# Attention: row sums in the maxima's banks, three banks for scores, maxima one at a time and later in a tile

## What is computed

```python
q = rms_norm(x @ w_q.T + b_q, g_q)        # 512 x 32
k, v         # 1344 text rows, masked beyond a length
k_img, v_img # 257 image rows
def attention(q, k, v, mask=None):
    s = einsum('bqhd,bkhd->bhqk', q, k) * SCALE
    p = softmax(where(mask, s, -1e9), axis=-1)
    return einsum('bhqk,bkhd->bqhd', p, v)
out = attention(q, k, v, mask) + attention(q, k_img, v_img)
```

## Time and profile before

| | us |
|---|---|
| median of three runs | 3357.7 |
| profiled execution | 3349.82 |
| its span, first to last instruction | 3347.8 |
| PE busy | 3063.8 |
| DVE busy | 2053.6 |
| ACT busy | 1606.9 |
| POOL busy | 1376.9 |

### The profile page before, as it was taken

The page is one execution under the profiler, slowest core; times in us unless marked ns, Lnnn a source line. Parts: engine busy times, 40 slices in busy tenths (PEclk is TensorE's granted clock), DMA queues, the critical chain, the costliest instruction groups (busy, mean ns, idle before and its releaser), DMA issues. The chain is left out here.

```text
span 3347.8 us, 49752 instructions
## 1 busy us (share of the span) xinstructions
PE 3063.8 (92%) x15756; PEld 1888.5 (56%) x15756; DVE 2053.6 (61%) x3425; ACT 1606.9 (48%) x3005; POOL 1376.9 (41%) x545
## 2 busy tenths in 40 slices
PE   7999999999599999999999999999994488999991
PEld 6777777777344444444444444444441466777771
DVE  5666766666566666766766666667652774443435
ACT  3343433434166666666666666666663653222222
POOL 0000000000087787877877877778775161000000
PEclk9999999999599999999999999999996699999996
DMA  5666667676846466465565564664633361000005
GB/s 170 157 163 166 163 162 169 160 150 159 169 83 132 104 127 126 97 128 124 107 133 106 125 132 99 125 127 100 133 55 108 93 203 44 1 1 0 0 0 201
DMA packets 374881, 385.16 MB, mean 115 GB/s; under 512 B 47792, under 2 KB 297712, under 8 KB 368504
## 3 DMA queue, kind: packets, MB, share of 16 engines
q1 hardware_dynamic: 363272, 323.61, 40.7%
q0 software_dynamic: 7168, 50.34, 8.5%
q10 hardware_dynamic: 4224, 8.39, 0.7%
HBM read 210.77 MB, written 121.15 MB: 99 GB/s over the span
## 5 line engine op out<-in xcount | busy, mean ns | idle before, releaser
L962 ACT ACTIVATE at_probs<-at_st 128x512 f32<-128x512 f32 (+1 forms) x1664 | 914.0, 595 | 614.5 <-PE at_st L812 599.0
L992 DVE TENSOR_REDUCE at_cm<-at_mx 128x2 f32<-128x896 f32 x768 | 813.1, 1087 | 432.1 <-PE at_mx L828 432.1
L772 POOL TENSOR_TENSOR at_added<-at_added,at_probs 128x2048 f32<-128x2048 f32 x192 | 888.6, 4628 | 11.5
L812 PE MATMUL at_st<-at_qst,at_kst 101*128 101x512 f32 (+1 forms) x1664 | 656.0, 456 | 6.2 <-ACT at_probs L962 5.7
L812 PEld LDWEIGHTS at_st<-at_qst,at_kst 101*128 101x128 f32 (+1 forms) x1664 | 265.9, 184 | 597.4 <-ACT at_probs L962 454.1
L828 PE MATMUL at_mx<-at_kst,at_qst 97*128 97x448 f32 (+1 forms) x2048 | 530.1, 362 | 50.1 <-DMA at_kst<-stack_rows 23.2
L850 PE MATMUL at_acc<-at_probs,at_vt 128*32 128x512 f32 (+2 forms) x3584 | 478.3, 608 | 0.7 <-ACT at_probs L962 0.7
L828 PEld LDWEIGHTS at_mx<-at_kst,at_qst 97*128 97x128 f32 x2048 | 371.3, 194 | 158.6 <-DVE at_cm L992 77.4
L740 POOL MEMSET at_ones<- 128x32 f32 x1 | 0.1, 130 | 819.1 <-POOLq L302 819.1
L772 POOL TENSOR_TENSOR at_added<-at_probs 128x2048 f32<-128x2048 f32 x32 | 146.6, 4581 | 325.9 <-ACT at_probs L962 325.9
L1508 ACT ACTIVATE ff_h<-ff_psa,ff_b1c,alpha 128x512 f32<-128x512 f32 x128 | 99.5, 778 | 344.6 <-PE ff_psa L1485 344.6
(11 more groups left out here) (203 smaller groups left out, 4701.5 us busy)
## 6 DMA issues: line engine op xcount, KB each, us to landing
at_kst<-k_high SPq DMA_DIRECT2D x256, 200.0 KB
at_probs<-at_probs POOLq DMA_DIRECT2D x32, 1024.0 KB, 7.0
at_kst<-k_low SPq DMA_DIRECT2D x128, 200.0 KB
pj_xin<-in_ctx_dram SPq DMA_DIRECT2D x96, 256.0 KB, 4.2
k_high<-pj_kh SPq DMA_DIRECT2D x96, 256.0 KB, 3.1
k_low<-pj_kl SPq DMA_DIRECT2D x96, 256.0 KB, 4.7
values<-pj_vs SPq DMA_DIRECT2D x96, 256.0 KB, 4.6
at_vt<-values SPq DMA_DIRECT2D x32, 768.0 KB
```

The costliest lines, as they stand in the source:

```text
L772: pool.tensor_tensor(added[:], so_far, probs[:, SLOT[t]], ALU.add).then_inc(S["add_done"], 1)
L812: pe.matmul(st[0:kn, h % 2, :], kst[g.j][:, h, t * P:t * P + kn], qst[g.j][:, h, :], start=True, stop=True).then_inc(S["st_done"], 1)
L962: act.activation(probs[0:kn, SLOT[t], h, :], st[0:kn, h % 2, :], ACT.Exp, scale=SCALE).then_inc(S["exp_done"], 1)
L992: dve.tensor_reduce(dst, mx[:, 2 * slot:2 * slot + 2, 0:kn], AX.X, ALU.max, negate=last).then_inc(S["mx_free"], 1)
```

## The change

- `acc` has one bank instead of two, scores have three instead of two. A score waits for the exponential three before it instead of two before it; the values now wait for all four exponentials of their tile themselves.
- The sums are written into banks of `mx`, between the maxima. There are two double blocks instead of five single ones: tile 6 and `added` at the end of tile 1 of the next group, tile 12 and tile 11 at the end of tile 2.
- The text half of tile 10 has no block of its own: a third DMA (`fold` 1) adds it into `added` after POOL's last addition.
- The 64 maxima of a group are single matmuls with a wait and a reduction each. In most tiles they stand behind the third score (two) and the fourth (three), in tiles 1 and 2 behind every score. 14 of the group after next stand in tiles 11 and 12.
- The ring's slots are dealt anew: tile 9 takes the slot of tile 4, tile 0 of the next group that of tile 9.

```diff
-    FOLDS = [(5, 0, P, 6), (10, HALF, P, 11)]
-    SUMMED = [(6, 0, P), (10, 0, HALF), (None, 0, P), (12, 0, KLAST), (11, 0, P)]
-    SUMS_AT = {10: [0], 11: [1]}
-    SUMS_LATE = {0: [2], 1: [3], 2: [4]}
+    FOLDS = [(5, 0, P, 6), (10, 0, HALF, None), (10, HALF, P, 11)]
+    SUMMED = [[(6, 0, P), (None, 0, P)], [(12, 0, KLAST), (11, 0, P)]]
+    SUMS_AFTER = {1: 0, 2: 1}
-    EARLY = 5
+    EARLY = 14
-    SLOT = [0, 1, 2, 3, 4, 5, 0, 1, 2, 3, 4, 5, 3]
+    SLOT = [0, 1, 2, 3, 0, 1, 2, 4, 5, 0, 3, 4, 5]
-        st, mx, acc = a.banks("st", 2), a.banks("mx", 4), a.banks("acc", 2)
+        st, mx, acc = a.banks("st", 3), a.banks("mx", 4), a.banks("acc", 1)
+        def spread(tiles, step, singles):
+            places = [(t, at) for t in tiles for at in ((0, 1, 2, 3) if t in SUMS_AFTER else (2, 3, "end", "end"))]
...
             def add(g, n):
                 elif not g.first:
-                    pool.wait_ge(S["s_done"], NSUM * g.at(-1).G + SUM_IMG0)
+                    pool.wait_ge(S["s_done"], 2 * g.at(-1).G + 1)
...
             def fold(g, n):
+                if into is None:
+                    pool.wait_ge(S["add_done"], NADD * (g.G + 1))
+                    dst = added[r0:r1]
...
             def body(g):              # POOL
                     add(g, n)
+                fold(g, 1)
                 if not g.first:
                     scale(g.at(-1))
-                fold(g, 1)
+                fold(g, 2)
...
             def scores(g, t, h):
-                    pe.wait_ge(S["exp_done"], n - 1)
+                    whole = h == 1 and t and PASS[t - 1][1:] != (0, P)
+                    pe.wait_ge(S["exp_done"], n - 1 if whole else n - 2)
...
             def values(g, q):
+                if r1 - r0 == P or t == KT - 1:
+                    pe.wait_ge(S["exp_done"], NST * g.G + HG * (t + 1))
...
+            def sums(g, q, bank):
+                if q == 0:
+                    pe.wait_ge(folded[0], 16 * (g.G + 1))
+                    pe.wait_ge(folded[1], 16 * (g.G + 1))
+                    pe.wait_ge(S["add_done"], NADD * (g.G + 1))
+                else:
+                    pe.wait_ge(folded[2], 16 * (g.G + 1))
+                for k, (t, r0, r1) in enumerate(SUMMED[q]):
+                    for h in range(HG):
+                        done = pe.matmul(mx[cols, bank, :], ones[r0:r1, :], src, start=k == 0, stop=k == 1)
...
             def reduce(w, m, start=False):   # DVE
-                dve.tensor_reduce(dst, mx[:, 2 * slot:2 * slot + 2, 0:kn], AX.X, ALU.max,
-                                  negate=last).then_inc(S["mx_free"], 1)
+                dve.tensor_reduce(dst, mx[:, bank % 4, 0:kn], AX.X, ALU.max, negate=last).then_inc(S["mx_free"], 1)
```

More of the change, by code:

```diff
@@ L673, in attend @@
         plan = {}
[L674 to L680, removed]
-        spread(range(TOPS[0] + 1, KT), 2, range(EARLY))
+        def spread(tiles, step, singles):
+            places = [(t, at) for t in tiles for at in ((0, 1, 2, 3) if t in SUMS_AFTER else (2, 3, "end", "end"))]
+            for n, m in enumerate(singles):
+                plan.setdefault(places[n * len(places) // len(singles)], []).append((step, m))
@@ new lines, in attend @@
+        spread(range(TOPS[0]), 1, range(EARLY, NMAX))
+        spread(range(TOPS[0] + 1, KT), 2, range(EARLY))
+        units = []
+        for t in range(KT):
+            for at in (0, 1, "values", 2, 3, "sums", "end"):
+                units += [("single",) + single for single in plan.get((t, at), [])]
+                if at == "sums" and t in SUMS_AFTER:
+                    units.append(("sums", -1, SUMS_AFTER[t]))
+        place = {unit: n for n, unit in enumerate(units)}
+        TOPS_AFTER = max(n for n, unit in enumerate(units) if unit[0] == "single" and unit[1] == 1)
@@ new lines, in runs, with bank_before @@
+        def runs(g, unit):
+            kind, step, _ = unit
+            return not (kind == "sums" and g.first) and g.followed(step)
+        def bank_before(g, n):
+            for body, top_n in ((g, n), (g.at(-1), len(units))):
+                known_start = body.known and body.G < 0
+                if known_start:
+                    there = [k for k in range(top_n) if units[k][:2] == ("single", 2)]
+                else:
+                    there = [k for k in range(top_n) if runs(body, units[k])]
+                there = [k for k in there if k % 4 == n % 4]
+                k = there[-1] if there else None
+                tops_between = top_n > TOPS_AFTER and (k is None or k <= TOPS_AFTER) and body.followed(1)
+                if tops_between:
+                    return ("tops", body.at(1), n % 4 // 2)
+                if k is not None:
+                    kind, step, m = units[k]
+                    return (kind, body.at(step), m)
+            raise ValueError("a bank without an earlier use")
@@ L852, in values @@
                 done.then_inc(S["v_done"], 1)
[L854 to L860, removed]
[L861 to L868 removed]
+            def sums(g, q, bank):
+                if q == 0:
+                    pe.wait_ge(folded[0], 16 * (g.G + 1))
+                    pe.wait_ge(folded[1], 16 * (g.G + 1))
+                    pe.wait_ge(S["add_done"], NADD * (g.G + 1))
+                else:
+                    pe.wait_ge(folded[2], 16 * (g.G + 1))
+                for k, (t, r0, r1) in enumerate(SUMMED[q]):
+                    for h in range(HG):
+                        cols = slice(h * HD, (h + 1) * HD)
+                        src = added[:, h, :] if t is None else probs[r0:r1, SLOT[t], h, :]
+                        done = pe.matmul(mx[cols, bank, :], ones[r0:r1, :], src, start=k == 0, stop=k == 1)
                 done.then_inc(S["s_done"], 1)
@@ L896, in body @@
                         ahead(g, t, h)
[L897 to L901, removed]
+                    if t in SUMS_AFTER and not g.first:
+                        n = place["sums", -1, SUMS_AFTER[t]]
+                        bank_free(g, n)
+                        sums(g.at(-1), SUMS_AFTER[t], n % 4)
                     ahead(g, t, "end")
             pe.wait_ge(S["const_set"], NC)
-            for m in range(NPAIR):
-                for r in range(2):
-                    maxima(Group(0, 0), m, r)
+            for m in range(NMAX):
+                if m >= 4:
+                    pe.wait_ge(S["mx_free"], m - 3)
+                maxima(Group(0, 0), m, m % 4)
             for half in range(2):
@@ L1016, in body @@
                 if not g.last:
-                    for m in range(0 if g.first else EARLY, NPAIR):
+                    for m in range(0 if g.first else EARLY, NMAX):
                         reduce(g.at(1), m)
```

111 lines of the change are left out of this document (63 added, 48 removed).

## The result

| | before | after |
|---|---|---|
| median of four runs, us | 3357.97 | 3311.16 (3307.42 to 3314.12) |
| profiled execution, us | 3349.82 | 3314.12 |
| its span, us | 3347.8 | 3312.3 |
| a group (first addition to first addition), mean of all 31, us | 51.18 | 49.81 |
| the same from the fifth group on, mean of 26, us | 51.31 | 49.94 |

The change is faster by 46.8 us, ratio 0.9856 (95% interval 0.9844 to 0.9869). The forecast was 73.6 us. By the profiled spans it is 35.5: 31 periods give 42.4, the start takes back 5.0 and the tail 1.9. The remaining 11 us are differences between executions: the profiled one is the slowest of the four after, and the one before lay 7.6 us under the fastest of its four. The 51.24 us of the forecast is a mean of 27 periods, the last of which, at the end of the loop, took only 49.22.

What follows compares the result with a forecast made beforehand. The prediction took a loop of POOL's additions, the new fold and PE's sums as the bound: 48.8 us a group against 51.24. 31 x 2.44 = 75.6, less 2, saves 73.6 us: 3357.7 - 73.6 = 3284, range 3255 to 3315.

Steps and rivals of the forecast that it cites:

- two of its own signs: PE idle about 2 us a group before the sums, released by a DMA; `mx` bank waits above 2 us would refute.
- The waits for exponentials go: Scores in tiles 3 to 9: PE's late waits for exponentials, 7 x 0.48 = 3.4 us a group, disappear.
- PE alone needs 46.5 us: PE by itself, per group: 51.24 less 1.3 for sums and 3.4 for exponential waits gives 46.5 us.
- A maximum now and then waits for its bank, 0.3 us a group, bounds 0 and 2: Five single maxima in a middle tile: occasional bank waits, 0.3 us a group, hidden below the 48.8 us loop.
- The loop through the third fold, 48.8 us: POOL's additions, fold into `added`, PE's sums, next addition: 38.26 + 0.1 + 8.2 + 2.05 + 0.2 = 48.8 us a group.
- the second rival: PE keeps waits in another form, at the 64 maxima: group 49.7 to 50.5 us, about 3320 us; chance 0.13.
- The start: The first group's 64 maxima run before anything else at DVE's pace: 2 us more.
- a rival: Slower: the new fold gets stuck in the loads; a landing of 11.5 us gives 3388 us; chance 0.09.
- The rule weighed against it: GpSimd-issued DMA: about 2.0 us fixed plus bytes at 436 GB/s, 3.2 us for 512 KB; loop 43.8 us, no bound.

Runs made afterwards that it cites:

- light reductions and no third fold: The change with only 64 columns of each bank reduced and half of tile 10 summed on PE instead of folded by DMA; 3218.99 us.
- without the third fold: The change with no DMA into `added`; half of tile 10 summed on PE as an extra block at the end of tile 1; 3322.59 us.
- light reductions: The change with each reduction reading only the first 64 columns of its bank, so maxima cover part of the keys; 3291.09 us.
- loads waiting: The change with SyncE's loads of the next stack starting only after the last fold of the group before has landed; 3305.41 us.
- second sums later: The change with the second double block of sums moved from the end of tile 2 to the end of tile 3; 3304.12 us.
- even places without the third fold: The change with maxima behind every score in tiles 1 to 9 and half of tile 10 summed on PE instead of folded; 3288.05 us.
- even places alone: The change with the maxima of tiles 3 to 9 behind every score instead of in the later half, third fold kept; 3301.7 us.
- the run at 3273.81 us: The change with no DMA into `added`, maxima behind every score in tiles 1 to 9, spread in tile 12, and 11 early maxima instead of 14; 3273.81 us.

## Why the prediction was right in sign and too large

The time lies in the stated range, but near its slow end, and not for the range's reason: 3255 to 3315 stood for a fold landing in 7.2 to 9.2 us, it landed in 7.9, and by the same sum that gives about 3275. By two of its own signs the mechanism was wrong: in most groups PE shows no DMA wait at the sums of tile 1, where 2 us were forecast, and the waits for `mx` banks come to more than 2 us a group. That 3311 us still fell inside is in part luck. Term by term:

*The waits for exponentials go.* Right: the earlier trace rows has 0.94 for the pair, after has 0.56. By the run with two banks the new order did it, and the third bank helps mainly where ACT copies the maxima (with the open end named there).

*PE alone needs 46.5 us.* With light reductions and no third fold it takes 47.4 on average with an extra block of 1.1, so 46.3 in the change's form: the sum was right for a PE that waits for nothing.

*A maximum now and then waits for its bank, 0.3 us a group, bounds 0 and 2.* This is the term that failed. Between the runs without the third fold, with full and with light reductions, lie 49.9 - 47.2 = 2.7 us a group, outside my bounds. I had compared DVE's load with the tile's length (3.1 against 3.1 us at worst) and not with the 1.05 us in which PE would start five maxima in four banks. And I took its price to be hidden under a loop of 48.8 us; with PE at 48.6 to 48.8 by itself there was no room left to hide anything.

*The loop through the third fold, 48.8 us.* Its pieces measured 38.3, 0.6 (for 0.1), 7.9 (for 8.2) and about 2.05, which gives 49.1 with the same 0.2. It exists: light reductions laid it bare, at 49.1 where the clock held. In the change it lies level with PE's own work and shows in 7 of 26 groups. The chance I gave the second rival, that PE keeps waits in another form (about 3320 us), was the better part of the truth.

*The last fold.* Not in the sum at all, and I gave no reason for leaving it out. Behind the third fold its landing went from 8 us to 12.4, and PE stood 0.5 us a group for it at the end of tile 2. It makes a second ring, over two groups. From a group's first addition to the sums behind its last fold are 53.3 us (the issue at 40.7, the landing 12.4 to 12.5 later, 0.13 to start). From there PE's own work, bank waits included, takes 45.7 to the first addition two groups on. That is 99.0, or 49.5 a group, longer than the 49.1 of the forecast's ring.

*The start.* 2 us forecast, 5.0 measured: the first scores came at 908.58 after 906.74 (DVE's pace, 1.8), the rest behind them. In the first tile PE has 19 instead of 14 maxima, and the clock is at half until 922 us instead of 917.

*The granted clock.* Not in the sum either: three groups at 52.1 us on average, 0.3 us a group spread over all.

*A slip in a rival.* For a landing of 11.5 us the loop passes 51.24 by 0.87 us, so 27 us and not 28; nothing hangs on it.

*The rule weighed against it.* The new fold took 7.7 us at least and 7.9 in the median. The Trainium skill's rule ("DMA: Bandwidth & Descriptors", section "Anatomy of one DMA — SWDGE (gpsimd) path") gave 3.2 us by an estimate and no loop; the trace does not agree, and the measurement decides.

Put together for a group: 46.3 for PE alone, 2.7 for banks, and 1.0 by which tiles 0 to 2 lie in the mean above their lowest (of which 0.5 is the wait for the last fold and 0.3 the clock): 50.0 us, measured 49.9. The terms come from different runs.

## What to carry to other kernels

Compare a producer and a consumer over a burst, not over a tile: four banks, five matmuls in 1.05 us and a reduction every 0.55 us cost 2.7 us of 50, though the reducing engine was idle 28% of the time. When three limits lie within 1 us of each other (here PE 48.8, a DMA ring 49.1, the ring through the late fold 49.5), taking one away brings little: a group (mean of all 31) went from 49.8 to 50.0 without the third fold, to 49.7 with light reductions, and to 47.4 with both. Count the groups in which the clock fell before comparing two runs: five such groups hid a gain of half a microsecond a group in one experiment, and their absence made up more than half of another's. Before putting a DMA between a sum and its use, add up the whole ring of who waits for whom, and the landing of the DMA queued behind it too.

## What the runs showed of the hardware

- Two adding DMAs of 512 KB that GpSimd issued 1.8 us apart landed 7.9 and 12.4 us after their issues; without the first of them the second took 8.2. Keeping the loads away took 0.9 us off the 12.4 and nothing off the 7.9.
- TensorE's granted clock stood at 1.00 from 917 to 2538 us before, and between 950 and 2400 us fell to 0.50 for 3.4 to 10 us at a time in eight of the eleven kernels with the change. With light reductions PE stood 1.4 to 2.9 us in front of the sums of tile 1 in every group, and all 17 falls between 950 and 2400 us came in or just behind such a wait; 11 of 26 waits had no fall.
- Other falls had shorter pauses in front of them. In the change one of three falls came behind waits of 0.39 and 1.40 us. The other two came about 2 us into tile 0 of the first group of a loop turn, where PE had stood only 0.32 and 0.38 us, and so did all those with loads waiting (5), second sums later (2), two banks (3) and even places without the third fold (3), and four of six with even places alone. In the kernel before and in the run at 3273.81 us, which had no fall, PE doesn't stand there that long (below 0.1 us). The run without the third fold stood there for 0.33 to 0.41 us, and its one fall came only at 2420 us, so the pause alone does not decide it; what does stays open. Two more came with light reductions and no third fold, at 2319 and 2363 us, in the 31st of 32 groups.
- A fall of 6.8 us made a group about 3 us longer: 52.2 after 49.2 us with loads waiting, 52.2 after 49.0 with even places and no third fold.
